# Two-layer transformer on one core: how many blocks of the second attention's maximum the first FFN does, and in what order

## The reference, cut to what matters

```
scores = jnp.einsum('bhqd,bhkd->bhqk', q, k) * SCALE
probs = jax.nn.softmax(scores, axis=-1)
attn = jnp.einsum('bhqk,bhkd->bhqd', probs, v)
```

## Time and profile before

| | us |
| --- | --- |
| median of 3 runs (lowest, highest) | 1518.24 (1513.48, 1519.17) |
| the profiled execution: its own time | 1520.89 |
| the profiled execution: its span | 1519.1 |
| first FFN, second to fourth down products and what lies between, to the last values | 588.5 to 697 |
| blocks only, then the first scores | 697 to 721 |
| second attention's steps with blocks | 721 to 1304 |
| second attention's steps without blocks | 1304 to 1352 |

### The profile page before, as it was taken

The page is one execution under the profiler, slowest core; times in us unless marked ns, Lnnn a source line. Parts: engine busy times, 40 slices in busy tenths (PEclk is TensorE's granted clock), DMA queues, the critical chain, the costliest instruction groups (busy, mean ns, idle before and its releaser), DMA issues. The chain is left out here.

```text
span 1519.1 us, 35666 instructions
## 1 busy us (share of the span) xinstructions
PE 1390.8 (92%) x13548; PEld 584.6 (38%) x13548; DVE 1186.1 (78%) x1530; ACT 1033.9 (68%) x1976; POOL 344.4 (23%) x472
## 2 busy tenths in 40 slices
PE   6888898999899899996999999999999999989998
PEld 3543333333333255441233333333333333236665
DVE  6686797888796044899999979997999789717766
ACT  3254676777688833221899989998999889964443
POOL 2501130300100033124140028301400040055225
PEclk9997899999999999997899999999999999999999
DMA  7821120111000003223200200000000000012454
GB/s 227 162 35 40 47 72 25 38 33 50 1 2 2 1 15 71 49 39 65 91 7 7 54 7 7 7 7 6 7 7 7 7 2 2 5 67 88 143 156 145
DMA packets 56868, 68.53 MB, mean 45 GB/s; under 512 B 9819, under 2 KB 52379, under 8 KB 55963
## 3 DMA queue, kind: packets, MB, share of 16 engines
q1 hardware_dynamic: 53635, 57.87, 14.7%
q0 software_dynamic: 3072, 8.39, 1.8%
HBM read 45.26 MB, written 26.74 MB: 47 GB/s over the span
## 5 line engine op out<-in xcount | busy, mean ns | idle before, releaser
L1854 DVE TENSOR_REDUCE mpart<-psum 128x2 f32<-128x1024 f32 (+2 forms) x832 | 913.0, 1157 | 91.8 <-PE psum L1265 74.0
L1582 ACT ACTIVATE probs<-psum 128x512 f32<-128x512 f32 (+1 forms) x1512 | 771.9, 573 | 157.2 <-PE psum L1301 84.2
L1326 PE MATMUL psum<-probs,v_region 128*17 128x256 f32 (+1 forms) x6400 | 502.9, 387 | 18.6 <-ACT probs L1576 9.3
L1265 PE MATMUL psum<-key_region,row_region 50*128 50x512 f16 (+3 forms) x1664 | 323.3, 381 | 46.8 <-DVE mpart L1854 36.7
L1301 PE MATMUL psum<-row_region,key_region 52*128 52x512 f16 (+3 forms) x1664 | 341.5, 380 | 17.6 <-ACT probs L1582 11.9
L1301 PEld LDWEIGHTS psum<-row_region,key_region 52*128 52x128 f16 x1664 | 93.9, 93 | 335.8 <-ACT probs L1582 264.4
L1326 PEld LDWEIGHTS psum<-probs,v_region 128*17 128x17 f32 x6400 | 107.1, 95 | 220.8 <-issue 114.3
L1060 POOL TENSOR_SCALAR mp<-mx 128x16 f16<-128x16 f32 x32 | 10.3, 322 | 647.7 <-DVE mx L1865 617.3
L1265 PEld LDWEIGHTS psum<-key_region,row_region 50*128 50x128 f16 x1664 | 94.8, 94 | 149.2 <-DVE mpart L1854 85.6
L1576 ACT ACTIVATE probs<-psum 128x1024 f32<-128x1024 f32 (+3 forms) x76 | 69.7, 955 | 11.0 <-PE psum L1301 8.5
L1617 ACT ACTIVATE probs<-psum,gate_s 128x512 f32<-128x512 f32 (+1 forms) x24 | 16.4, 682 | 64.9 <-PE psum L1369 64.9
(11 more groups left out here) (196 smaller groups left out, 1358.8 us busy)
## 6 DMA issues: line engine op xcount, KB each, us to landing
parts<-key_region SPq DMA_DIRECT2D x32, 256.0 KB, 3.0
key_region<-parts SPq DMA_DIRECT2D x48, 128.0 KB, 4.3
sorted_x<-in_zero SPq DMA_DIRECT2D x46, 128.0 KB, 2.6
key_region<-sorted_x SPq DMA_DIRECT2D x46, 128.0 KB
sorted_y<-key_region SPq DMA_DIRECT2D x46, 128.0 KB
row_region<-parts SPq DMA_DIRECT2D x144, 32.0 KB
key_region<-in_wmod SPq DMA_DIRECT2D x2, 1536.0 KB, 11.6
x_sb<-in_x SPq DMA_DIRECT2D x4, 512.0 KB, 8.3
```

The source lines that it names most:

```text
L1265: mm = pe.matmul(bank(b + par)[:, 0:w], rows[at, g, hp, r * P:(r + 1) * P], keys[at, g * HP + hp, q * CH:q * CH + w], start=True, stop=not ...
L1326: mm = pe.matmul(psum[32 * h:32 * h + VW, SUM_BANK, lo:hi], v_sb[:, jt, g * HG + h, :], probs[:, (S0[y] + s) % 2, h, lo:hi], start=(jt == ...
L1582: nc.scalar.activation(probs[:, (S0[y] + s) % 2, 2 * hp + par, off:CH], psum[:, e % 3, off:CH], ACT.Exp, scale=SCALES[y]).then_inc(s_p, 1)
L1854: V.tensor_reduce(mpart[:, n % NG, at:at + 2, q:q + 1], psum[:, b:b + 2, 0:w], AX.X, ALU.max).then_inc(drained(*item)[0], 1)
```

## The change

The list of early blocks is made unit by unit, and within a unit key chunk by key chunk; before, key chunk 0 of the four first units came ahead of the others. In the first FFN most places get one block where they had two. So 31 blocks are done there in place of 52: 24 of unit 0 (key chunks 0 to 2) and 7 of unit 1, where it was 24 of unit 0, 12 of unit 1 and 8 each of units 2 and 3. `attention_walk` takes the other 21. Behind the last down product (`st` 2 3) there stands a block of unit 0 with key chunk 2, where there was one with key chunk 1; behind the last values there are 5 blocks, where there were 7.

```diff
--- before.py
+++ after.py
@@ -250,8 +250,7 @@
 def early_blocks():
 
 
-    first = [b for n in range(HG) for b in pairs_of(1, n) if b[5] == 0]
-    return first + [b for n in range(HG) for q in range(1, NCH - 1) for b in pairs_of(1, n) if b[5] == q]
+    return [b for n in range(HG) for q in range(NCH - 1) for b in pairs_of(1, n) if b[5] == q]
 
 
 def hidden_pair(y, tc, c):
@@ -297,18 +296,16 @@
 
         p = tc - 1
         for c in range(NC[0]):
-            out.append(("hg", 0, tc, c))
-            blocks(1)
-            out.append(("hid", 0, tc, c))
+            out += hidden_pair(0, tc, c)
             blocks(1)
             if c == 0:
                 out += [("dn", 0, p, 0), ("sa", 2, p)]
                 if tc > 2:
                     loaded[0] = p
-                blocks(2)
+                blocks(1)
                 out.append(("dn", 0, p, 1))
                 loaded[0] = p
-                blocks(2)
+                blocks(1)
                 out.append(("st", 2, p))
             if tc == 1 and c == 3:
                 project_keys(p, 1)
@@ -329,20 +326,20 @@
     loaded[0] = p - 1
     for z in range(2):
         out.append(("dm", 0, p, z))
-        blocks(2)
+        blocks(1)
         out.append(("dn", 0, p, z))
         if z == 0:
             out.append(("sa", 2, p))
-            blocks(2)
+            blocks(1)
     out.append(("st", 2, p))
     loaded[0] = p
     blocks(1)
     out += [("qk", 1, p - 1, 0), ("nm", 2, p), ("ql", 1, p - 1, 0), ("v", 1, p - 1), ("ln", 2, p)]
-    blocks(4)
+    blocks(2)
     project_keys(p, 1)
     project_rows(p, 1)
     out.append(("v", 1, p))
-    blocks(7)
+    blocks(5)
     return out, done
```

## The result

The changed kernel takes **1530.9 us** in the median of four runs (1528.5 to 1533.7); the kernel before, beside it, 1517.2 (1513.5 to 1519.2). The ratio is 1.0079 [1.0049, 1.0109]: slower by 0.8%. The forecast was 1536.6, in a range from 1522 to 1543, with slower by over 0.5% at 0.74. Sign, place and most of the sizes came as forecast; the sum was some 2 us too high in the stages and some 6 in the whole.

The account below looks back on a forecast made before the run. VectorE was taken to bound the second attention by a hair, PE the first FFN. Gains of 9.0 us less 3.6 and 3.3 leave 2.1; against 20.6 the change costs 18.5, giving a median of 1536.6 us, range 1522 to 1543.

Parts of the forecast that it names:

- attention, 21 blocks: Second attention: each of 21 added blocks costs VectorE 1.14 us, partly absorbed by its stalls; +20.6 us, between 17.4 and 23.8.
- FFN loop, 14 blocks and waits: First FFN, third and fourth chunk's loops: 14 blocks give back PE's 0.325 us each, and normalisation waits shrink by 1.85; -6.4 us.
- three blocks out of the down products: End of the first FFN's loop: three times 0.325 us, and PE's 0.74 wait for a reduction goes; -1.7 us.
- wait for chunk 2's keys, less the low parts: Behind the last down product: PE waits 4.2 us for key copies, 0.6 comes back at the transposes; +3.6 us.
- clock: Behind the new key wait PE's clock halves for 6.6 us before it comes back; +3.3 us, ends 0 and 8.
- two blocks ahead of the last projection: First FFN's end: blocks run inside a wait for features, so removing them gives nothing; 0.65 us if the cover were gone.
- tail: Behind the last values: two fewer reductions give 2.3 us, late copy of the last keys takes back 1.35; -0.9 us.
- Rival 1: Second attention: PE holds the pace, VectorE has slack; 0.325 us per added block, 6.8 in all, 1519.6 us; chance 0.15.
- rival 2: First FFN's loop follows VectorE, so its 14 blocks give 16.0 us, not 6.4; 1520.2 to 1527.1 us; chance 0.1.
- rival 3: First FFN's end: chunk 2's key copies land in time, no wait, no clock fall; +11.6 us, 1529.8; chance 0.15.
- rival 4: Second attention: third blocks delay a unit's maximum, scores wait for row copies; +3 to +6 us on the forecast; chance 0.1.

Follow-up runs that it names:

- the repeat: The changed kernel profiled and measured once more, unaltered, beside the kernel before on the same chip: ratio 1.0073 [1.0057, 1.0089].
- the second pair: Profiles of the kernel before and the changed kernel, each run once more unaltered: first FFN and attention together 781.8 and 795.2 us.
- unchanged_again: The kernel before, unaltered, measured once more like the other runs: ratio 0.9986 [0.9968, 1.0004].
- order_alone: The kernel before with only the new unit-by-unit order of blocks, 52 blocks at the old places: ratio 1.0014 [0.9993, 1.0034].
- normalise_first: The kernel before, 52 blocks kept, normalisation moved ahead of blocks in the FFN loops of chunks 2 and 3: 1520.8 us against 1525.7, ratio 0.9968.
- keys_later: The changed kernel with the block behind the last down product taking key chunk 0, chunk 2 used only behind the last transposes: ratio 1.0053 [1.0030, 1.0075].
- busy_wait: The changed kernel with part of the last down product done three times, so PE works through its wait for keys: ratio 1.0066 against the kernel before.
- loops_alone: The kernel before, old order, with only the 14 blocks taken out of the third and fourth chunk's FFN loops: ratio 1.0018 [1.0000, 1.0036].
- more_reductions: The kernel before with VectorE's reduction of 21 second-attention blocks done twice: ratio 1.0171 [1.0143, 1.0199].
- more_matmuls: The kernel before with the matmul pair of 21 second-attention blocks done twice: ratio 1.0030 [1.0007, 1.0053].
- six_more: normalise_first with 6 blocks more in the first FFN's loops, 58 in all, and the key order of keys_later: ratio 1.0008 [0.9997, 1.0020] to the kernel before.
- first_and_busy: The kernel before with the edits of normalise_first and busy_tail together: ratio 0.9975 [0.9958, 0.9993].
- busy_tail: The kernel before with the matmul pair of 20 blocks between the last values and the first scores done three times: ratio 0.9986 [0.9970, 1.0002].

## Why the prediction was right, step by step

The pair of profiles is before and changed, if nothing else is said. The first FFN's stretches are read off PE's timelines of the two profiles, from instruction to instruction.

| step | forecast | measured |
|---|---|---|
| attention, 21 blocks | +20.6 | +21.4 (+20.1 in the repeat) |
| FFN loop, 14 blocks and waits | -6.4 | -9.6 |
| three blocks out of the down products | -1.7 | -1.7 |
| wait for chunk 2's keys, less the low parts | +3.6 | +3.5 |
| clock | +3.3 | +4.0 (2.6 at this wait, 1.4 at the next) |
| two blocks ahead of the last projection | 0 | -0.3, and see the clock |
| tail | -0.9 | -0.6 |
| stages together | +18.5 | +16.9 (0.1 more ahead of the loop) |

**The attention: right**, in size and in engine. Of the 3.2 us that I let VectorE's stalls absorb, 1.7 were absorbed (1.4 in the second pair), and not where I had put them: the 0.49 of each unit stayed, and the 1.7 went out of all waits. So the middle that I took between 17.4 and 23.8 had no reason of its own, and that it came so near is in part luck. The profiles with unedited attention work (before, unchanged_again, order_alone, normalise_first against the changed kernel's two, keys_later and busy_wait) give +20.6 in the mean, from 18.8 to 23.1.

**The FFN loop: right in mechanism, mis-sized by 3.2 us**, and this is the term that was furthest off. Two things were wrong in it. I had left 1.0 us of the 1.37 wait in each chunk, because PE would arrive earlier too; measured, the waits of the earlier trace rows and their like in the other chunk (3.8 us in all) went altogether. With the block gone from ahead of it VectorE is early enough. loops_alone shows the same without the other parts of the change, and normalise_first removes the waits by order alone, with all 52 blocks in place. And a block between gate and up costs PE more than the 0.325 from its start to the next: the six gate products run 1.40 us with a block behind them and 1.30, from 588.91 to 590.21, with the up products. With 0.42 for each of the eleven blocks taken from there, about 0.3 for the other three and the 3.8 of waits, the sum is 9.3 of the 9.6. A third thing is in no single pair: with the waits goes the chance that the clock falls behind them. From the down products of chunk 1 to the keys' projection of chunk 2 the six profiles with the old loop take 72.5 to 76.1 us, 74.5 in the mean, and the five with the new one 63.1 to 63.8, 63.3 in the mean. By these means the loop gives 11.2, and the 9.6 came from a profile of before in which the clock had stayed up.

**The new wait: right**, 4.15 where 4.2 was worked out. The sum had the loop's saving on both sides, in PE's arrival and in the keys' landing, so its mis-size did no harm; only the 1.7 of the down products moved PE against the copies. keys_later gives back 6.1 to 7.1 where wait and clock of the forecast were 6.9.

**The clock: right for the wrong pause in part.** It fell behind the wait for keys as forecast, and it cost 2.5 us in that projection and 0.2 in the block ahead of it (the values behind took 0.1 less than before), where I had 3.3; the window from 665 on has 1.00 again, 6.0 us after the wait's end, against the 6.6 that I had taken. The other 1.4 arose at the last projection, where I had written that two blocks fewer cost nothing. **That is the step that failed in kind**: I had asked only whether the blocks' time was hidden, and the pause that they had broken up (1.11 and 0.74 us) became one of 2.33. The cover is not the whole cause. Ten profiles keep the blocks and their pauses there. In five the clock stayed up (before, unchanged_again, more_reductions, more_matmuls, six_more), in five it fell: order_alone, loops_alone, normalise_first, first_and_busy and busy_tail, with 2.70 to 3.60 us for the first eight matmuls. busy_tail runs the unaltered code up to there. So what the two blocks bought was a chance, and how much of the 1.4 their absence costs is open.

**The tail: right.** The late copy of chunk 3's keys is there: 2.55 us of PE, 1.61 of VectorE where 1.35 was forecast, and 0.6 was gained of the 2.3 that two blocks are worth.

**The whole.** The stages gave +16.9 and +13.4 in the two pairs of profiles, the ratios 11 to 12 with upper ends at 13.6 and 16.5. The forecast's 18.5 was 1.6 too much by its own profiles, mainly the loop's 3.2 less what the clock and the attention had more. Part of the gap between stages and ratios is the profile of before: its clock fell nowhere in the loop, which happened in only one other of the six profiles with that loop. With the means, an FFN of 192.8 us in the four profiles of unaltered code and 187.0 in the two of the changed one, and +20.6 for the attention, the stages give +14.8, inside the first ratio's interval and 1.2 above the second's. The 3 to 4 us that remain are not explained. A gap of this size the other way stands in more_reductions, with +26 by the ratio and 22.3 by the stages.

Rival 1 falls by more_matmuls, rival 2 by the loop's 9.6 to 11.2 against its 16.0 (though half as much again as I took, or more), rival 3 by the wait of 4.15 us in the changed kernel and by keys_later, rival 4 by more_reductions, which accounts for the attention without any late maximum.

## What to carry to other kernels

Where two engines are both busy for 98%, their shares don't say which of them holds the pace: repeat a piece of each one's work a few times and read what it costs, and also take some away, for at a corner between engines the price upward says nothing of the price downward. When filler work is reordered, look at what each piece reads and when that lands; here one line's place (keys_later) is worth 6 to 7 us of the first FFN. Before taking filler out, try to move the late work ahead of it: normalise_first made the kernel faster by 0.3% without giving up a block. And take more than one profile of the kernel before: one in which the clock happens to stay up makes every change look worse.

## What the runs showed of the hardware that was not expected

**The same pause costs the clock in one run and not in another.** Six profiles have the old loop with its two pairs of waits. Behind 1.14 and 0.64 us the clock stayed up in four of them and fell in two; behind 1.37 and 0.64 us it stayed up in two and fell in four (2.48 to 2.74 us for six matmuls in place of 1.47). The kernel before and unchanged_again, which are one kernel, stand on different sides both times. Behind the pauses of 1.11 us and the one after it, at the last projection, it was five to five. The waits of 2.33 us behind the transposes lost it in all four profiles that have them, the changed kernel's two, keys_later and busy_wait.

**That also moves the whole time.** Up to the first marker the kernels are the same, yet this takes from 518.9 to 529.2 us. Two windows of the first attention in the kernel before:

```profile
160.00:180.00 20.00, 17.37 (x170) 7.17 (x171) 13.62 (x20) 10.99 (x25) 3.21 (x6) 0.76 0.19 54
260.00:280.00 20.00, 18.12 (x200) 7.56 (x192) 13.45 (x13) 13.68 (x31) 7.22 (x8) 0.78 0.10 28
```

and in unchanged_again, the same code, 6.8 us quicker to the marker:

```profile
160.00:180.00 20.00, 16.84 (x214) 7.08 (x210) 16.49 (x21) 14.97 (x32) 3.13 (x5) 1.00 0.18 55
260.00:280.00 20.00, 18.10 (x232) 7.12 (x230) 17.53 (x19) 15.79 (x35) 7.22 (x8) 1.00 0.18 52
```

A granted clock of 0.76 and 0.78 against 1.00 and 1.00. These are the two windows of 20 us that differ most; over the whole stretch the means are 0.95 and 0.97. All 14 profiles follow that: a mean of 0.97 goes with 518.9 and 522.0 us to the marker, 0.96 with 522.1 to 525.2, and 0.95 with 525.4 to 529.2. A difference of under 10 us between two profiles of this kernel means nothing until it is cut into stages.
